# Gated linear attention and ternary FFN on one core: four rows of K, Q and products in one VectorE operation, and other call orders

## The reference

```python
q = (x @ Wq).reshape(b, s, H, HD); k = ...Wk; v = ...Wv
fg = jax.nn.sigmoid(x @ Wf + bf)
def step(state, inp):
    qt, kt, vt, gt = inp
    state = state * gt[..., None] + vt[..., None] * kt[..., None, :]
    out_t = jnp.einsum('bhij,bhj->bhi', state, qt)
...
out = layernorm(out) * gamma + beta
out = (out * jax.nn.silu(x @ Wg)) @ Wout
x = layernorm(x + out)
# FFN, weights w are ternary, each product is scaled per output feature
h = silu(x @ w1 * s1) * (x @ w2 * s2)
h = gelu(h @ h1 * sh1); h = gelu(h @ h2 * sh2)
x = layernorm(x + h @ w3 * s3)
```

## Time and profile before

| | |
|---|---|
| median of 3 runs | 525.56 us |
| lowest and highest | 523.36 and 525.65 us |
| span of the profiled execution, first to last instruction | 520.7 us |
| busy TensorE, VectorE, ScalarE, GpSimd | 502.3, 453.9, 403.9, 317.8 us |
| DMA | 87.33 MB, 168 GB/s |
| granted TensorE clock, mean | 0.999 |

### The profile page before, as it was taken

One profiled execution on the slowest core, in us unless ns is written; L12 is line 12 of the kernel. 1 busy time (PEld: TensorE's weight loads), 2 busy tenths in 40 slices (PEclk: granted clock), 3 DMA queues, 4 the chain that ended last, 5 costly groups with the idle time before them and its releaser, 6 DMA issues. The chain is left out here.

```text
span 520.7 us, 7950 instructions
## 1 busy us (share of the span) xinstructions
PE 502.3 (96%) x2524; PEld 382.6 (73%) x2524; DVE 453.9 (87%) x707; ACT 403.9 (78%) x837; POOL 317.8 (61%) x363
## 2 busy tenths in 40 slices
PE   8999999999999999999999999999999998999995
PEld 5466777787876767787877777687767777767885
DVE  4699899999999998999999989999998999991462
ACT  3567778789797688889888787889788878678754
POOL 0642755839394765938295775858496775838351
PEclk9999999999999999999999999999999999999999
DMA  6987998972998748895597963699947747400001
GB/s 197 257 230 165 250 230 217 230 166 77 211 232 218 174 133 199 211 237 162 128 233 196 265 167 70 166 228 234 237 108 196 180 131 177 107 1 2 21 22 43
DMA packets 21500, 87.33 MB, mean 168 GB/s; under 512 B 2512, under 2 KB 3280, under 8 KB 13520
## 3 DMA queue, kind: packets, MB, share of 16 engines
q1 hardware_dynamic: 21312, 86.53, 66.7%
q10 hardware_dynamic: 144, 0.26, 0.1%
HBM read 74.72 MB, written 12.06 MB: 167 GB/s over the span
## 5 line engine op out<-in xcount | busy, mean ns | idle before, releaser
L474 POOL TENSOR_TENSOR h1lo<-h,h1hi 128x512 fp32r<-128x512 f32 x60 | 77.7, 1313 | 27.4 <-ACT h1hi L891 27.1
L898 ACT ACTIVATE h<-F,cols 128x512 f32<-128x512 f32 x120 | 79.0, 686 | 9.4 <-PE F L2303 8.9
L542 POOL TENSOR_TENSOR QJ<-QJ 128x512 f32<-128x512 f32 x14 | 18.0, 1285 | 102.6 <-DVE QJ L1589 102.6
L474 POOL TENSOR_TENSOR h2lo<-h,h2hi 128x512 fp32r<-128x512 f32 x60 | 76.1, 1298 | 5.6 <-ACT h2hi L891 5.5
L1574 DVE TENSOR_TENSOR_SCAN KJ<-g,KJ 128x512 f32<-128x512 f32 x64 | 74.8, 1203 | 3.7 <-POOL KJ L523 3.2
L1574 DVE TENSOR_TENSOR_SCAN KJ<-g,carry,KJ 128x512 f32<-128x512 f32 x64 | 77.8, 1261 | 0.3 <-ACT carry L824 0.2
L2303 PE MATMUL F<-h2hi,whi 128*128 128x512 f32 (+1 forms) x256 | 73.4, 421 | 1.8 <-DVE h2hi L1694 1.0
L1581 DVE TENSOR_TENSOR QJ<-QJ,KJ 128x1024 f32<-128x1024 f32 x60 | 75.0, 1275 | 0.0
L2303 PE MATMUL F<-h1hi,whi 128*128 128x512 f32 (+1 forms) x256 | 69.8, 413 | 3.8 <-DVE h L1638 3.8
L2303 PE MATMUL F<-h1lo,whi 128*128 128x512 f32 (+1 forms) x256 | 67.1, 404 | 0.0
L2303 PE MATMUL F<-h2lo,whi 128*128 128x512 f32 (+1 forms) x256 | 66.0, 400 | 0.0
(11 more groups left out here) (176 smaller groups left out, 947.7 us busy)
## 6 DMA issues: line engine op xcount, KB each, us to landing
KJ<-qk_bounce SPq DMA_DIRECT2D x30, 1024.0 KB, 11.2
QJ<-qk_bounce SPq DMA_DIRECT2D x30, 1024.0 KB, 11.4
qk_bounce<-qk SPq DMA_DIRECT2D x30, 256.0 KB, 3.1
x_in<-in_x SPq DMA_DIRECT2D x16, 256.0 KB, 7.8
xT<-in_xT SPq DMA_DIRECT2D x15, 256.0 KB, 4.6
out<-res SPq DMA_DIRECT2D x15, 256.0 KB, 3.1
wraw<-in_wffn SPq DMA_DIRECT2D x2, 1024.0 KB, 10.5
wraw<-in_wffn SPq DMA_DIRECT2D x2, 256.0 KB, 4.3
```

Of the source, the lines that this page charges most:

```text
L474: e.tensor_tensor(h_lo[layer][:, t, :w], h[:, t, :w], h_hi[layer][:, t, :w].bitcast(f32), ALU.subtract).then_inc(lo_done[layer], 1)
L542: e.tensor_tensor(first, first, other, ALU.add).then_inc(add_gp_done, 1)
L898: e.activation(dst[:, t, :WIDTH[n]], F[t][:, :WIDTH[n]], ACT.Gelu, scale=scale[t]).then_inc(gelu_done[layer], 1)
```

## The change

The VectorE operations of K, Q and their products take four rows where they took two: kv takes rows 0 to 3 and then 4 to 5, qs rows 0 to 3 and 4 to 7, and the adds are 0..3 += 4..7 and 0..1 += 2..3. GpSimd keeps its last add and its rows of kv. kv_pairs becomes kv_vector, and the counts of waits follow.

The tables of waits that were defaults with exceptions (freed in TensorE's stream, load_xT in SyncE's) are written out in full; the conditions are the same, but for project_v, which counts kv operations, now two in a block.

All five engines get other call orders. The main shifts: on SyncE load_projections(1) goes behind the first x, weights and constants, and load_w3 comes early; on VectorE find_low_parts, half_norm("1"), scan(1, 7) and set_flag change places, qs(n, 0) stands between the scans in most blocks, kv(n + 1, 0) goes ahead of x1_lo(n) or hmul(n, 0) in most blocks; on TensorE project_v, transpose_y and attention_out come earlier among the FFN's products, project_k(4) goes ahead of sum_transposed(1), and transpose_x1(15) comes two mid_lo earlier; on ScalarE center_w3 and the first low sums come earlier; on GpSimd qsj_gp(1) goes ahead of kvj_gp(2), scale_w3 comes early, and rstd_of(15, "1") goes ahead of lo(2, 14, 2).

```diff
-    NPAIR = HD // 2
-    ADDS = 3
+    NQUAD = 2
+    ADDS = 2
...
-        def kv_pairs(n):
-            return sum(2 if m in EARLY else 3 for m in range(1, n))
+        def kv_vector(n):
+            return sum(1 if m in EARLY else 2 for m in range(1, n))
...
             def kv(n, p):
-                if p % 2 == 0:
-                    e.wait_ge(K_landed[p // 2][n % 2], fetched(n))
+
+                js = (slice(0, 4), slice(4, 6))[p]
+                e.wait_ge(K_landed[p][n % 2], fetched(n))
                 if p == 0:
 
                     e.wait_ge(v_copied, n + 1)
-                K = rows(KJ, n)[:, 2 * p:2 * p + 2, :]
-                vb = ps_v[:, :WIDTH[n]].unsqueeze(1).broadcast_to([P, 2, WIDTH[n]])
+                K = rows(KJ, n)[:, js, :]
+                vb = ps_v[:, :WIDTH[n]].unsqueeze(1).broadcast_to([P, js.stop - js.start, WIDTH[n]])
                 e.tensor_tensor(K, vb, K, ALU.mult).then_inc(kv_done, 1)
...
             def qs(n, p):
-                if p % 2 == 0:
-                    e.wait_ge(Q_landed[p // 2][n % 2], fetched(n))
-                e.wait_ge(scan_done, HD * n + 2 * p + 2)
-                Q = rows(QJ, n)[:, 2 * p:2 * p + 2, :]
-                e.tensor_tensor(Q, Q, rows(KJ, n)[:, 2 * p:2 * p + 2, :], ALU.mult).then_inc(qs_done, 1)
+                e.wait_ge(Q_landed[p][n % 2], fetched(n))
+                e.wait_ge(scan_done, HD * n + 4 * p + 4)
+                js = slice(4 * p, 4 * p + 4)
+                Q = rows(QJ, n)[:, js, :]
+                e.tensor_tensor(Q, Q, rows(KJ, n)[:, js, :], ALU.mult).then_inc(qs_done, 1)
 
             def add(n, p):
 
-                e.wait_ge(qs_done, NPAIR * (n - 1) + p + 2)
-                if p:
-                    e.wait_ge(add_done, adds(n) + p)
-                first, other = (rows(QJ, n)[:, 2 * k:2 * k + 2, :] for k in (0, p + 1))
+                if p == 0:
+                    e.wait_ge(qs_done, NQUAD * n)
+                else:
+                    e.wait_ge(add_done, adds(n) + 1)
+                r = HD // 2 >> p
+                first, other = (rows(QJ, n)[:, k:k + r, :] for k in (0, r))
                 e.tensor_tensor(first, first, other, ALU.add).then_inc(add_done, 1)
```

SyncE, the first transfers:

```diff
             load_projections(0)
+            load_x(0)
+            load_weights(0)
+            load_constants()
+            load_xT(1)
             load_projections(1)
-            load_xT(1)
-            load_x(0)
-            load_constants()
-            load_weights(0)
+            load_w3()
             load_xT(2)
```

GpSimd, the first calls:

```diff
             qsj_gp(0)
+            qsj_gp(1)
             kvj_gp(2)
-            qsj_gp(1)
+            kvj_gp(4)
             qsj_gp(2)
-            kvj_gp(4)
             qsj_gp(3)
+            scale_w3()
             kvj_gp(6)
             kv_gp(1, 4)
             kv_gp(1, 5)
+            kv_gp(1, 6)
             rstd_of(0, "o")
-            kv_gp(1, 6)
+            rstd_of(0, "1")
             kv_gp(1, 7)
-            rstd_of(0, "1")
-            scale_w3()
```

VectorE, the first blocks:

```diff
             spread_weights(1)
+            kvj(0)
             spread_weights(0)
-            kvj(0)
+            kvj(1)
             scan(0, 0)
-            kvj(1)
             scan(0, 1)
...
             kv(1, 0)
             qsj(7)
-            kv(1, 1)
+            scan(1, 0)
             stats_o(0)
-            scan(1, 0)
             scan(1, 1)
             half_norm("o")
...
             scan(1, 5)
+            find_low_parts()
             scan(1, 6)
-            find_low_parts()
+            half_norm("1")
+            scan(1, 7)
             set_flag()
-            half_norm("1")
+            x1_lo(0)
             qs(1, 0)
-            x1_lo(0)
-            qs(1, 1)
-            scan(1, 7)
-            qs(1, 2)
             hmul(0, 0)
             hmul(0, 1)
-            qs(1, 3)
+            qs(1, 1)
```

More of the change, by code:

```diff
@@ L571, in _ @@
             lo(1, 0, 2)
+            rstd_of(1, "o")
             lo(1, 0, 3)
-            rstd_of(1, "o")
             kv_gp(2, 6)
@@ L773, in _ @@
             lo(2, 13, 2)
+            rstd_of(14, "1")
             lo(2, 13, 3)
-            rstd_of(14, "1")
+            rstd_2(12)
             add_gp(15)
@@ L1018, in _ @@
             copy_q(2)
+            copy_v(2)
             silu(0, 0)
+            silu(0, 1)
+            g_of_tanh(2)
             save_carry(1)
-            silu(0, 1)
             hi(1, 0, 0)
-            g_of_tanh(2)
+            copy_q(3)
+            hi(1, 0, 1)
             silu(0, 2)
-            hi(1, 0, 1)
             silu(0, 3)
             hi(1, 0, 2)
+            copy_k(4)
             hi(1, 0, 3)
-            copy_q(3)
-            center_w3()
             norm_o(1)
@@ L1043, in _ @@
             norm_1(1)
+            gelu(2, 0, 0)
+            gelu(2, 0, 1)
+            x1_hi(1)
             save_carry(2)
[L1045 to L1047 removed]
             gelu(2, 0, 2)
@@ L1435, in _ @@
             hi(2, 12, 3)
+            copy_v(15)
+            tanh(15)
             norm_1(13)
+            gelu(2, 12, 0)
             x1_hi(13)
-            gelu(2, 12, 0)
             gelu(2, 12, 1)
@@ L1726, in _ @@
             scan(0, 4)
+            qsj(4)
             kvj(5)
-            qsj(4)
             scan(0, 5)
@@ L1797, in _ @@
             scan(3, 3)
+            kv(4, 0)
             residual_1(2)
+            scan(3, 4)
             stats_1(2)
-            scan(3, 4)
             scan(3, 5)
@@ L1881, in _ @@
             scan(6, 5)
-            residual_1(5)
-            stats_1(5)
             scan(6, 6)
             scan(6, 7)
+            residual_1(5)
+            qs(6, 0)
+            stats_1(5)
+            kv(7, 0)
+            scan(7, 0)
             qs(6, 1)
+            x1_lo(5)
             add(6, 0)
-            qs(6, 2)
-            x1_lo(5)
-            qs(6, 3)
+            scan(7, 1)
+            hmul(5, 0)
             add(6, 1)
-            add(6, 2)
-            hmul(5, 0)
             hmul(5, 1)
@@ L1911, in _ @@
-            scan(7, 6)
             scan(7, 7)
             qs(7, 1)
-            qs(7, 2)
+            kv(8, 0)
+            scan(8, 0)
             x1_lo(6)
-            qs(7, 3)
             add(7, 0)
+            hmul(6, 0)
             add(7, 1)
-            hmul(6, 0)
-            add(7, 2)
             hmul(6, 1)
             residual_2(5)
-            kv(8, 0)
+            scan(8, 1)
             hmul(6, 2)
@@ L2003, in _ @@
             residual_2(8)
-            kv(11, 0)
+            scan(11, 0)
             hmul(9, 2)
+            stats_o(10)
             hmul(9, 3)
-            stats_o(10)
-            scan(11, 0)
-            kv(11, 1)
-            kv(11, 2)
             scan(11, 1)
@@ L2057, in _ @@
             residual_2(10)
-            kv(13, 0)
+            scan(13, 2)
             hmul(11, 2)
@@ L2122, in _ @@
             scan(15, 4)
+            scan(15, 5)
             residual_1(14)
             stats_1(14)
-            scan(15, 5)
+            qs(15, 0)
             scan(15, 6)
             scan(15, 7)
-            qs(15, 0)
             qs(15, 1)
+            x1_lo(14)
             add(15, 0)
-            x1_lo(14)
-            qs(15, 2)
             add(15, 1)
-            qs(15, 3)
             hmul(14, 0)
-            add(15, 2)
             hmul(14, 1)
             residual_2(13)
+            stats_o(15)
             hmul(14, 2)
-            stats_o(15)
             hmul(14, 3)
@@ L2803, in rest @@
                 mid_hi(2, 8, 3, low_parts)
+                transpose_x1(9)
                 mid_lo(2, 8, 0, low_parts)
@@ L2849, in rest @@
                 mid_lo(2, 9, 2, low_parts)
+                transpose_x1(10)
+                project_q(13)
                 mid_lo(2, 9, 3, low_parts)
@@ L2899, in rest @@
                 up_lo(11, 2, low_parts)
+                up_hi(11, 3, low_parts)
+                up_lo(11, 3, low_parts)
                 sum_transposed(12)
-                up_hi(11, 3, low_parts)
                 project_k(14)
-                up_lo(11, 3, low_parts)
+                project_v(14)
                 mid_open(1, 11, 0, low_parts)
@@ L2939, in rest @@
                 up_hi(12, 2, low_parts)
+                up_hi(12, 3, low_parts)
+                sum_transposed(13)
                 up_lo(12, 2, low_parts)
-                up_hi(12, 3, low_parts)
                 up_lo(12, 3, low_parts)
                 project_gate(14)
-                sum_transposed(13)
+                project_v(15)
                 mid_open(1, 12, 0, low_parts)
```

1157 lines of the change are left out of this document (556 added, 601 removed).

## The result

The changed kernel takes 568.8 us (median of 4 runs, 568.6 to 569.6), beside 525.5 for the kernel before on the same chip: a ratio of 1.085, 95% interval 1.081 to 1.088. The profiled execution spans 567.0 us where the one before spans 520.7. The forecast was 522.2, so this is wrong in sign and by 46.6 us.

The account below looks back on a forecast made before the run. TensorE's own work was taken as the bound, to within 0.3 us of a 29.2 us period. 525.6 - 1.9 (start) - 1.5 (shorter hmul waits), moves at 0, gave 522.2 us, chance 0.43, range 517.2 to 527.5.

Parts of the forecast that it names:

- 59 operations fewer, 0.07 us each: VectorE's products, K*v and adds made wider: 4.1 us less VectorE work over the run, 0.27 a block.
- TensorE's wait for hmul would fall: Steady part: a lighter VectorE shortens TensorE's 3.5 us of matmul waits for hmul, 1.5 us of it taken.
- The start, -1.9 us: Block 0: half_norm earlier -1.2 us, hmul(0,0) earlier -1.1, later stats_o(0) +0.4; bounds -2.3 and +1.7.
- The lag of 1.3 us: Start: scan(0,2) about 1.3 us later behind GpSimd's reordered products, run out by scan(0,6), priced 0; otherwise costs 1.3 us.
- I price the moves themselves at 0: Steady part: reordered calls keep TensorE, ScalarE and GpSimd work the same, covered by TensorE's back-to-back products: 0 us.
- a saving of 1.5 us: Steady part: wider VectorE operations, a block 0.3 to 0.5 us lighter, shorten TensorE's waits for hmul by 1.5 us.
- Rival 3: SBUF port shared by VectorE and GpSimd: four-row products delay h2lo, 0.4 us a block, 529.6 us; chance 0.14.
- TensorE's busy time was to stay the same to 2 us: Whole run: a sign of being right, TensorE's busy time unchanged to 2 us.
- Fewer operations also mean fewer collisions: VectorE against GpSimd at the shared SBUF port: argument against the slower port case; no size given.
- The signs of being wrong: x1_lo distance above 29.3 us, new GpSimd operations over 2 us during h2lo, or first x1_lo later than 48.4 us.
- Where the forecast was said to fall most easily: The start, where 1.3 us of GpSimd lag behind its reordered products decides.

Follow-up runs that it names:

- micro-kernel: Separate kernel: eight GpSimd lo operations alone, then beside VectorE products of four, two and one rows; a GpSimd operation takes 1.2 us alone, 3.3 beside four rows.
- e8: Kernel before with the change's call order only until block 0's first up-products, old order behind that, widths as before: 526.8 us, ratio 1.005.
- e11: Changed kernel with its Q*K products cut to 64 of 512 columns, the rest left unmultiplied: 520.5 us, ratio 0.993.
- e2: Changed kernel with all its new orders, each four-row operation issued as two of two rows: 559.1 us, ratio 1.069.
- e6: Kernel before in its old orders, K*v, products and sums four rows wide, the second product ahead of x1_lo: 550.6 us, ratio 1.054.
- e7: Old orders, four-row operations, second product ahead of x1_lo, one product input replaced by the gate in PSUM: 541.0 us, ratio 1.036.
- e3: Changed kernel with its new orders, products and sums issued as four of one row, K*v left at four rows: 573.2 us, ratio 1.096.
- e5: Changed kernel with one product input the gate in PSUM instead of the state, plus a wait for ScalarE: 543.9 us, ratio 1.042.

## Why the prediction was wrong

- **59 operations fewer, 0.07 us each: right for the operation, wrong for the engine.** 648 for 707, 2.27 to 2.29 us for four rows undisturbed, 0.05 to 0.07 saved for each pair in the micro-kernel. But VectorE's busy time rose by 2.3 us, since its products now wait for GpSimd (2.51 us on average). That TensorE's wait for hmul would fall was right (1.2 us).
- **The start, -1.9 us: half right.** half_norm began 1.96 us earlier (44.33 us, 46.29 in the earlier trace rows) and hmul(0,0) at 49.67 where it was 52.44; x1_lo(0) 1.5 us earlier. The lag of 1.3 us did not come (scan(0,2) at 15.50, 0.5 us later). Over all profiles the first x1_lo comes at 46.8 to 48.9 us with the new start (ten, median 47.4) and at 47.0 to 48.8 with the old (eight, median 48.5), so about 1 us is gained, and as much again is scatter. e8 shows a collision with h1lo that gives it back.
- **"I price the moves themselves at 0": the step that failed.** I counted work by engine and let TensorE's back-to-back products cover the rest. The cover was GpSimd's 0.65 us of slack at h2lo and 0.6 us at the small operations. e11 shows that the moves are nearly free when the products are short; with full products they cost 36 us even at two rows (e2). The width failed at the same step. Its term was a saving of 1.5 us (from a block lighter by 0.3 to 0.5 us, where the forecast's own sum gives 0.27), on the ground that it comes off an engine that is not the bound; in the old orders the widths alone cost 28 us (e6).
- **Rival 3, right in kind and wrong in size.** I had found the port and gave 529.6 us and a chance of 0.14. Its price, 1.07 - 0.65 = 0.4 us a block, took the difference between a wide and a narrow hit. But in the old order there were few hits (GpSimd is 317.8 us busy there, and 311.1 in e7, where no product holds the port), so a new hit costs its whole 2.1 us. It took one hit a block, on h2lo. The small operations for 1/sigma are a chain of four, in which each can be caught anew, and h2lo queues behind them; kv_gp, gated_y and h1lo are hit as well. 53.5 us of GpSimd's time are 3.6 a block over 15 blocks, where I had 1.07, and the period grew by 3.1 us, where I had 0.4.
- **Not on the list at all:** that TensorE's stops cost it clock. TensorE's busy time was to stay the same to 2 us and rose by 12.3 for the same 2524 products, in part by the clock (0.974).
- **"Fewer operations also mean fewer collisions"**, my argument against rival 3, is refuted by e2: in the same orders it has 59 operations more than the change, GpSimd is busy for 358.6 us in place of 371.3, and it is 10 us faster. But fewer rows do not cure it either: e2 is still 36 us slow, and e3 no better than the change. As far as these runs show, the place against GpSimd's work decides how many hits there are, and the length what one costs.
- **The signs of being wrong** were well chosen: an x1_lo distance above 29.3 us came (32.3), and so did new h2lo over 2 us (11). Where the forecast was said to fall most easily, at the start, it did not fall.

What stays open is the split of the 43 us between the port and the length of the operations. By e5 the port is 23 or more in the new orders; e5's own wait hides the rest. In the old orders the port is the smaller part: e7 wins 9.6 of the 28 us that the widths cost there.

## What to carry to other kernels

Ahead of any move on VectorE, list for each two-SBUF operation what GpSimd does at that time, and price a new hit at the operation's whole length, for each link of a dependent chain. A tiny GpSimd operation is held as long as a big one: if such operations must stay on the critical chain, let the long operation wait for them; here that wait won 0.8% in the kernel before and 2% in the changed one. A merged operation saves 0.05 to 0.07 us and doubles what everything behind it in order may have to wait.

## What was not expected of the hardware

- A GpSimd operation over 4 elements a partition is held like one over 512: 2.25 and 3.05 us where it takes 0.20 and 1.01.
- In the micro-kernel the engines alternate, one operation each: 3.3, 2.2 and 1.7 us a GpSimd operation beside products of four, two and one rows. The Trainium skill (SBUF — State Buffer, "SBUF: two separate sides") speaks of an exclusive lock; these numbers agree. In the kernel an operation of GpSimd can miss its turn: one of 0.20 us was held for 4.39, across two products. A broadcast input in PSUM frees GpSimd altogether (9.83 us for eight, 9.80 alone).
- After a stop of 5.66 us TensorE's granted clock fell to 0.50 for 6 us and came back by 309 us; over the trace of before it is 1.00 from 60 to 440 us. That stop was paid for twice.
